# A graph layer's main loop: 108 instead of 96 chunks of edges summed on TensorE, by a schedule made at build time

## What is computed

```python
h = relu(layernorm(x))
xw = h @ W_in
W_ij = (shifted_softplus(edge_attr_20 @ W_f1 + b_f1) @ W_f2 + b_f2) * edge_weight1
x_ij = xw[dst] * W_ij
out = segment_sum(x_ij, src, 6250)
return x + shifted_softplus(out @ W_o1 + b_o1) @ W_o2 + b_o2
```

## Time and profile before

| | before |
|---|---|
| median of 3 runs | 2446.28 us (2439.71 to 2447.08) |
| the profiled execution | 2439.41 us, span 2437.6 us |
| busy, share of the span: PE, POOL, DVE, ACT | 87%, 79%, 73%, 71% |
| chain of work that ended last | DMA of the scatters 42%, POOL 22%, issue 21%, PE 8%, DVE 4% |
| scatters | 1180, of 1592 ns on average |
| mean granted TensorE clock | 0.966 of full speed |

### The profile page before, as it was taken

One profiled execution on the slowest core, in us unless ns is written; L12 is line 12 of the kernel. 1 busy time (PEld: TensorE's weight loads), 2 busy tenths in 40 slices (PEclk: granted clock), 3 DMA queues, 4 the chain that ended last, 5 costly groups with the idle time before them and its releaser, 6 DMA issues.

```text
span 2437.6 us, 54860 instructions
## 1 busy us (share of the span) xinstructions
PE 2132.0 (87%) x15903; PEld 1381.0 (57%) x16098; DVE 1790.4 (73%) x3773; ACT 1737.7 (71%) x4085; POOL 1935.9 (79%) x1240
## 2 busy tenths in 40 slices
PE   2688999999999998999999999999999999999935
PEld 1555556665556565555556555565565565555613
DVE  8667777777777777777777777777777777777747
ACT  1577777777777777777777777777777777777703
POOL 2388888888888888888888888888888888888863
PEclk9889999999999999999999999999999999999968
DMA  8366666666556665666566666565566566666564
GB/s 350 109 96 90 87 90 91 87 94 90 86 92 90 86 94 87 88 92 87 88 92 90 84 93 90 85 93 90 84 92 90 86 90 91 87 90 92 76 169 172
DMA packets 360143, 244.45 MB, mean 100 GB/s; under 512 B 90419, under 2 KB 347137, under 8 KB 359711
## 3 DMA queue, kind: packets, MB, share of 16 engines
q0 software_dynamic: 170912, 80.62, 35.4%
q1 hardware_dynamic: 187715, 159.83, 24.9%
q10 hardware_dynamic: 1212, 0.42, 0.1%
HBM read 141.43 MB, written 99.27 MB: 99 GB/s over the span
## 4 chain that ended last, share of the span: by engine, by line
DMA 42%; POOL 22%; issue 21%; PE 8%; DVE 4%; ACT 1%; POOLq 0%; ACTq 0%; SPq 0%; DVEq 0%
DMA acc<-region,target 42%; POOL acc L591 21%; PE ps L1276 2%; PE ps L1295 2%; PE ps L1255 1%; PE ps L1245 1%; PE ps L1262 1%; ACT region L713 1%; DMA w_f<-in_L_gnn_W_f_dram 1%; PE ps L1326 0%; POOLq L590 0%; DVE region L1150 0%; DVE mean L853 0%; DVE variance L861 0%; DVE region L1165 0%
## 5 line engine op out<-in xcount | busy, mean ns | idle before, releaser
L591 POOL DMA_INDIRECT acc<-region,target x1180 | 1878.8, 1592 | 376.6 <-issue 267.0
L1276 PE MATMUL ps<-region 128*128 128x386 bf16 x2688 | 580.9, 337 | 71.1 <-ACT region L722 70.4
L722 ACT ACTIVATE region<-ps 128x386 bf16<-128x386 f32 x672 | 331.6, 493 | 231.6 <-PE ps L1276 195.5
L1295 PE MATMUL ps<-region 64*128 64x448 bf16 x4032 | 453.4, 358 | 17.9 <-DVE region L1067 13.4
L745 ACT ACTIVATE region<-ps,cut_col 128x128 f32<-128x128 f32 x1564 | 440.3, 363 | 0.6 <-PE ps L1326 0.6
L1255 PE MATMUL ps<-w_f,region 128*128 128x128 f32 x3128 | 428.8, 282 | 13.1 <-issue 2.4
L1255 PEld LDWEIGHTS ps<-w_f,region 128*128 128x128 f32 x3128 | 427.8, 198 | 12.1
L1276 PEld LDWEIGHTS ps<-region 128*128 128x128 bf16 x2688 | 232.4, 97 | 315.6 <-ACT region L722 109.7
L1002 DVE SCALAR_TENSOR_TENSOR region<-ps,bf_negative,region 128x512 f32<-128x512 f32 x391 | 291.3, 745 | 123.8 <-ACT region L708 84.0
L993 DVE TENSOR_SCALAR moved<-region,weight_limit,spare_row 128x4 f32<-128x4 f32 x295 | 97.3, 330 | 374.3 <-ACT region L713 247.4
L1262 PE MATMUL ps<-region 128*128 128x129 f32 x2360 | 327.4, 279 | 28.9 <-DVE region L1002 24.5
(11 more groups left out here) (128 smaller groups left out, 1690.6 us busy)
## 6 DMA issues: line engine op xcount, KB each, us to landing
dst_b<-dst_rows SPq DMA_DIRECT2D x391, 128.0 KB
src_b<-src_rows SPq DMA_DIRECT2D x295, 128.0 KB
acc<-region,target POOLq DMA_INDIRECT x1180
attrT<-in_edge_attr_dram SPq DMA_DIRECT2D x782, 20.0 KB
acc<-region SPq DMA_DIRECT2D x20, 640.0 KB, 17.4
xwin<-xw_parts SPq DMA_DIRECT2D x391, 31.5 KB
region<-acc SPq DMA_DIRECT2D x48, 256.0 KB, 4.7
xw_parts<-parts SPq DMA_DIRECT2D x12, 384.0 KB, 2.3
```

What stands on the lines that cost most here:

```text
L591: nc.gpsimd.indirect_dma_start(out=acc[a], out_offset=bass.IndirectOffsetOnAxis(ap=target[:, slot, t:t + 1], axis=0), in_=summed[:, slot, ...
L722: nc.scalar.activation(binned[:, h, j, :], binned_ps[:, 0:PC], ACT.Copy).then_inc(s_binned, 1)
L1276: ins = MM(binned_ps[:, 0:PC], place[:, h % 2, t, j * P:(j + 1) * P], payload_high[:, h % 2, t, :], start=(t == 0), stop=(t == T - 1))
L1295: ins = MM(ps[6 + r][:, 0:NL], binned[rows, slot, j, part * F:(part + 1) * F], in_node[rows, i, slot, :], start=(d == every[0] and part == ...
```

## The change

The period becomes 25 chunks with seven of them on PE, cut off at 108, of which the last is chunk 384. The distances between PE chunks are 3 and 4 in turn. 283 pool chunks are left of 295. The fixed tables give way to a loop that runs while the kernel is built and assigns every sort, one-hot, half node sum and add to a step: at most two sorts per step (one early, one late; `late` is a sort's position), at most one half of a node sum, its one-hots two steps ahead, and the add one step behind the second half. A sort comes no sooner than 3 steps after its chunk and after its slot is free. The place matrices come two at a time. `in_node` takes turns by the number of the tile, and `local_f` shares the memory of `bin_i`. The order of each engine's code within a step stays.

```diff
-U = 16
-ON_PE = (3, 7, 11, 15)
+U = 25
+ON_PE = (2, 6, 9, 13, 16, 20, 24)
+NPE = 108
...
-        BINNED_AT = {4: (0,), 5: (1, 2), 6: (3, 4), 7: (5, 6)}
         OLD, NEW = (3, 2), (1, 0)
-        NODES_AT = ((4, 0, OLD), (5, 0, NEW), (6, 1, OLD), (7, 1, NEW))
-        DENSE_AT = ((6, 0, OLD), (7, 0, NEW), (8, 1, OLD), (9, 1, NEW))
-        ADDED_AT = ((8, 0), (10, 1))
-        PLACED_AT = ((0, (0,)), (2, (1,)), (3, (2, 3)))
-        LAST_DENSE = max(pe_index) + DENSE_AT[1][0]
-        EXTRA = 2 * (SLOTS - 1)
+        PLACED_AT = ((0, (0, 1)), (2, (2, 3)))
+        SORTS_PER_STEP = 2
...
+        def tiles_summed(kk):
+            return range(2 if kk % SLOTS < SLOTS - 1 else 1)
+
+        sorts_at, nodes_at, sums_at, adds_at = ({} for _ in range(4))
+        sorted_in, summed_in = {}, {}
+        turn, last = (0, 0), 0
+
+        def next_turn(t):
+            return (t[0], 1) if t[1] == 0 else (t[0] + 1, 0)
+
+        for kk in range(NPE + SLOTS - 1):
+            for i in range(JT if kk < NPE else 0):
+                j = tile_of(kk % SLOTS, i)
+                earlier = kk - ((kk - 1 - j // 2) % SLOTS + 1)
+                freed = (summed_in[earlier, j % 2], 1) if kk >= SLOTS else (0, 0)
+                turn = max(next_turn(turn), (pe_chunks[kk] + 3, 1), freed)
+                sorted_in[kk, i] = turn
+                sorts_at.setdefault(turn[0], []).append((kk, kk % SLOTS, i, turn[1]))
+            for i in tiles_summed(kk):
+                for ages in (OLD, NEW):
+                    for d in ages:
+                        if holds(kk, d):
+                            step, late = sorted_in[kk - d, place_of((kk - d) % SLOTS, tile_of(kk % SLOTS, i))]
+                            ready = max(ready, step + 2 + late) if d != ages[0] and holds(kk, ages[0]) else step + 2 + late
+                    if any(holds(kk, d) for d in ages):
+                        last = max(last + 1, ready)
+                        nodes_at.setdefault(last - 2, []).append((kk, kk % SLOTS, i, ages))
+                        sums_at.setdefault(last, []).append((kk, kk % SLOTS, i, ages))
+                summed_in[kk, i] = last
+                adds_at.setdefault(last + 1, []).append((kk, kk % SLOTS, i))
...
-                    for kk, h, i in dense_jobs(k, ADDED_AT, 1):
+                    for kk, h, i in adds_at.get(k, ()):
...
-                    for job in dense_jobs(k, DENSE_AT, 0):
+                    for job in sums_at.get(k, ()):
                         add_nodes(*job)
-                    for job in jobs[1:]:
-                        bin_up(*job)
+                    for kk, h, i, late in jobs:
+                        if late:
+                            bin_up(kk, h, i)
```

More of the change, by code:

```diff
@@ L35, in gnn_kernel @@
     LN2 = math.log(2.0)
-    NU = NCH // U
-    NPE = NU * len(ON_PE)
     NL = N // BINS
@@ L42, in gnn_kernel @@
     PC = 3 * F + 2
-    NQU = len(ON_PE)
     BANK_QCS = NPE // 3
     assert all((n >> 6) * SEVENTH >> 11 == n // NL for n in range(N))
-    assert N == BINS * NL and NL % 64 == 0 and NL <= 512 and NPE % 4 == 0 and NPE == 3 * BANK_QCS and BANK_QCS * BINS <= 512
-    assert NQU % SLOTS == 0 and JT == 2 * SLOTS - 1
+    assert N == BINS * NL and NL % 64 == 0 and NL <= 512 and NPE == 3 * BANK_QCS and BANK_QCS * BINS <= 512
+    assert JT == 2 * SLOTS - 1
     acc = [nc.dram_tensor(f"acc{t}", (ACC_ROWS, F), fp32, kind="Internal").ap() for t in range(ACCS)]
@@ L101, in gnn_kernel @@
         pe_src, bin_i, bit_i = (region1[:, 2 * G * CE + k * NPE * T:2 * G * CE + (k + 1) * NPE * T].bitcast(i32).rearrange("p (n t) -> p n t", t=T) for k in range(3))
-        bin_f, local_f = (region1[:, 2 * G * CE + k * NPE * T:2 * G * CE + (k + 1) * NPE * T].rearrange("p (n t) -> p n t", t=T) for k in range(3, 5))
-        assert 5 * NPE * T <= G * CE
+        bin_f = region1[:, 2 * G * CE + 3 * NPE * T:2 * G * CE + 4 * NPE * T].rearrange("p (n t) -> p n t", t=T)
+        local_f = bin_i.bitcast(fp32)
+        assert 4 * NPE * T <= G * CE
         region2 = sb("region2", [P, max(NB * F, 4 * ACCS * EB * F, 14 * CE + 6 * T)])
@@ L294, in known @@
             return type(c) is int
-        pe_index = {c: kk for kk, c in enumerate(c for c in range(NU * U) if c % U in ON_PE)}
+        pe_chunks = [c for c in range(NCH) if c % U in ON_PE][:NPE]
+        pe_index = {c: kk for kk, c in enumerate(pe_chunks)}
+        assert len(pe_chunks) == NPE
         pe_counts = [0] + list(itertools.accumulate(int(c in pe_index) for c in range(NCH)))
@@ L355, in sums_until @@
             return JT * (kk // SLOTS) + 2 * (kk % SLOTS) + i + 1
[L357 to L377, removed]
@@ L382, in nodes_until @@
+        c = last
+        LAST_STEP = max(NCH + 1, c + 2)
         def nodes_until(kk, i, ages):
             behind = [d for d in OLD + NEW if d < ages[-1]]
-            jobs = [(q, r) for q in range(kk + 1) for r in range(2 if q < kk else i + 1) if 2 * (q % SLOTS) + r < JT]
+            jobs = [(q, r) for q in range(kk + 1) for r in tiles_summed(q) if q < kk or r <= i]
             return sum(1 for q, r in jobs for d in OLD + NEW if holds(q, d)) - sum(1 for d in behind if holds(kk, d))
         def hybrid_steps(step):
-            for c in range(-2, max(NCH + 2, LAST_DENSE + EXTRA + 3)):
+            for c in range(-2, LAST_STEP + 1):
@@ L731, in step @@
                         take_sums(n % 4)
-                    jobs = binnings(k)
-                    for job in jobs[:1]:
-                        take_binned(*job)
+                    jobs = sorts_at.get(k, ())
+                    for kk, h, i, late in jobs:
+                        if not late:
+                            take_binned(kk, h, i)
                     n = k + 1
@@ L910, in bins @@
                 for r, k in enumerate(ON_PE):
-                    last = V.tensor_copy(pe_src[:, :, :].rearrange("p (u r) t -> p u r t", r=len(ON_PE))[:, :, r, :],
-                                         src_int[:, 0:NU * U, :].rearrange("p (u k) t -> p u k t", k=U)[:, :, k, :])
+                    n = len(range(r, NPE, len(ON_PE)))
+                    last = V.tensor_copy(pe_src[:, r:NPE:len(ON_PE), :], src_int[:, k:k + (n - 1) * U + 1:U, :])
                 link(last)
@@ L1059, in step @@
                             places(k - off, tiles)
-                    for kk, h, i, ages in dense_jobs(k, NODES_AT, 0):
+                    for kk, h, i, ages in nodes_at.get(k, ()):
                         j = tile_of(h, i)
@@ L1066, in step @@
                                 wait(dve, s_binned, (kk - d) * JT + place_of(slot, j) + 1)
-                                V.tensor_scalar(in_node[:, i, slot, :], counting[:, 0:NL], binned[:, slot, j, 3 * F:3 * F + 1],
+                                V.tensor_scalar(in_node[:, sums_until(kk, i) % 2, slot, :], counting[:, 0:NL], binned[:, slot, j, 3 * F:3 * F + 1],
                                                 binned[:, slot, j, 3 * F + 1:PC], ALU.subtract, ALU.is_equal).then_inc(s_node, 1)
@@ L1294, in add_nodes @@
                             rows = slice(r * CAP, (r + 1) * CAP)
-                            ins = MM(ps[6 + r][:, 0:NL], binned[rows, slot, j, part * F:(part + 1) * F], in_node[rows, i, slot, :],
+                            ins = MM(ps[6 + r][:, 0:NL], binned[rows, slot, j, part * F:(part + 1) * F], in_node[rows, sums_until(kk, i) % 2, slot, :],
                                      start=(d == every[0] and part == 0), stop=(d == every[-1] and part == 2))
```

## The result

| | before | after |
|---|---|---|
| median | 2446.68 us (4 runs, 2439.71 to 2447.84) | 2495.85 us (4 runs, 2490.62 to 2496.93) |
| the profiled execution | 2439.41 us, span 2437.6 | 2496.54 us, span 2494.7 |
| busy: PE, POOL, DVE, ACT | 87%, 79%, 73%, 71% | 89%, 75%, 74%, 71% |
| scatters | 1180 | 1132 |

The changed kernel is slower by 49.2 us: ratio 1.0203, 95% interval 1.0179 to 1.0227. The forecast was 2481, its range 2455 to 2525.

What follows compares the result with a forecast made beforehand. PE was taken to bound the loop instead of POOL: profiled 2439.4 us, + 36.1 for the loop, + 3 half clock, + 3 prologue, - 4 tail = 2477.5; with half of the 6.9 median offset 2481, range 2455 to 2525.

Steps and rivals of the forecast that it cites:

- What bounds: Main loop: POOL's scatters bound before, PE after; 370 stretches on PE sum to 2080.5 us without late adds.
- The four kinds of stretch: PE between hidden products: 243 full at 5.69 us, 103 without sums 5.56, 15 one sort fewer 5.3, 9 without node sum 5.07.
- The added wait: PE's node sum waits 1.2 us for an add to accT behind DVE's payload, 51 times, 61 us; bounds 1.0 and 1.5.
- The drain: DVE between payload and add: the rows show no pause, so the sum leaves out the skill's rule of about 0.8 us.
- E: Rival: DVE pauses behind the two long payload instructions, 0.8 us more per wait, 2522 us; chance 0.02.
- Half clock: PE at 1.2 GHz after waits: two cases of 1.6 each, 3 us; bounds none and all 51 (82 us).
- Prologue and tail: Before and after the loop: VectorE's bin and rank work adds 3 us, the tail takes 4 off (bounds 0 and 9).
- The sum: Whole kernel: profiled execution 2439.4 + 36.1 + 3 + 3 - 4 = 2477.5 us, then half of 6.9 for the median: 2481.
- A: Rival: the add to accT is not late, as DVE begins earlier or PE's node sum is late too; 2420 us, chance 0.10.
- C: Rival: POOL still bounds, with PE faster in full steps than read; 2355 us, chance 0.03.
- D: Rival: a bin of 14 holds more than 64 edges of a chunk, so the general branch runs; unpriced, chance 0.01.
- One sign: Expected in the changed profile: ACT's L712 no longer waits for acc; no size given.

Runs made afterwards that it cites:

- e5: e1 with the fourth scatter of every pool chunk left out on POOL: 2426.10 us, where e1 has 2426.47.
- e6: Kernel before with the fourth scatter of every pool chunk left out: 2357.34 us, ratio 0.9659 to the kernel before.
- e1: Changed kernel with the adds to accT moved ahead of the payload in DVE's step: 2426.47 us, ratio 0.9944 to the kernel before.
- e3: Changed kernel with the adds to accT one place later, behind the comparison of duplicates: 2570.09 us (two runs).
- e4: Changed kernel with the adds ahead of the payload only for PE chunks of even running number: 2467.84 us, ratio 1.0117 to the kernel before.
- e2: Kernel before with the adds to accT moved ahead of the payload, as a control: 2441.53 us, ratio 1.0005.
- e7: e1 with 102 chunks on PE, four of every 15: 2426.06 us, ratio 0.9937 to the kernel before.
- e9: e1 with the early sort behind the hidden product in steps without same-source sums: 2424.30 us, ratio 0.9935 to the kernel before.

## Why the prediction was right, and where its sizes were off

**What bounds.** POOL before, PE after: right, by e5 and e6. PE's need in the loop, without the late adds, was put at 2080.5; the changed kernel's 2160.8 less 51 x 1.50 is 2084.3. The four kinds of stretch held: 5.70 for 5.69, 5.55 for 5.56, 5.02 for 5.07, and 5.53 for the 5.3 that I had taken between two ends.

**The added wait.** Right in place, cause and count: 51 in the 370 stretches, and e1, e3 and e4 move the time with it. The size was put at 1.2, upper bound 1.5, and measured 1.50 (7.053 - 5.553), so 76.5 us instead of 61.2. This term alone makes most of the miss. Its parts: L1002 starts 0.11 behind the hidden product in all 51, as taken; from there to the add 2.23 us (on average, 2.07 to 2.43) for the 2.07 read from one case; the add 1.08, as taken; and 0.15 from its end to PE's first matmul, which I had put into the bound and not into the value. The 2.07 was the shortest: over the 96 payload steps of the kernel before the same chain takes 2.07 to 2.46, 2.16 on average. One row for a chain of short instructions was too thin.

**The drain.** E, by which DVE would pause 0.8 us more ahead of the add, would have made the wait 2.3 with the measured rest. The rows show none: in the stretch above L1051 starts at 368.60, 0.03 behind the end of L1049, lasts 0.69, and L1060 starts at 369.21. E took one sentence of the Trainium skill (VectorE: DVE Perf Modes, The DRAIN you can't avoid) alone; the same paragraph adds that a next instruction that isn't held back starts earlier. The trace agrees with that for L1060, which starts 0.08 before L1051's end.

**Half clock.** Taken as 3 us, was 0 in the 370 stretches. e3 shows that the mechanism is there. The prediction's reading that none ran at half clock behind a wait up to 1.36 was wrong: five stretches without a node sum did, which began with waits of 0.29 to 1.08, each with another wait of 0.83 to 1.31 in the stretch before it. One of them, on PE in the kernel before, where the filter product takes 1.91 instead of 1.05:

```profile
596.22 0.70 PE L1245 MATMUL ps<-attrT,w_f 20*128 20x256 f32 x4 [1.08 <-ACT region L712]
...
597.67 1.91 PE L1255 MATMUL ps<-w_f,region 128*128 128x128 f32 x8 [0.22 <-issue]
```

The other premise, that the new wait of 1.2 lies under the 1.42 where the clock began to fall, went with the size of the wait: 26 of the 51 are 1.42 or longer. That the clock held in all 51 is luck as far as the prediction goes.

**Prologue and tail.** +3 was +7.0 up to step 16. The first hidden product of the loop comes at 98.40 instead of 92.29. The three steps on 1512 instead of 1344 columns (the prediction had two) account for 2.1 us (4 x 0.17 each); I had bounded the whole at 5. The value is itself unsteady: that product comes at 92.1 to 92.4 in the four traces with 96 chunks on PE, and at 96.4 to 98.4 in the six with 108. Where the rest comes from is open. The tail gave 5.1 for the 4 taken, though e2, with the tail of the kernel before, is 2.0 longer there than that kernel, so a us or two is chance. The early gain of the scatters was lost to the reload of x, as said: L1140, the former L1131, ran from 2417.42 to 2424.11, and the tail's first add began at 2424.15 behind it.

**The sum.** +36.1 + 3 + 3 - 4 = 38.1 was forecast between the profiled executions, and 57.1 measured: 15.3 from the size of the wait, 3.8 from the other stretches, 4.0 from the prologue, less 3 for the clock and 1.1 for the tail. The 3.4 that the forecast added from profiled execution to median did not come: the median of after lies 0.7 below its profiled execution. Rivals A and C fell with L1060's waits and POOL's slack. D did not happen. One sign came only in part: ACT's L719 (L712 before) still waits 90 times for a scatter from 300 to 2200 us, but 0.4 at most, where it had waited up to 3.2.

## What to carry to other kernels

When a schedule is made by a program, the order inside a step is part of it: the old tables kept the adds out of the payload's step, and the new loop, which counts only what PE does per step, lost that unwritten rule. Read the old distances for what they avoid, step by step on every engine, before replacing them. And when work moves from the bounding engine to the next, compare the limits first: the kernel before had 3.4% to give by e6, but moving 12 chunks to PE brings only 13.4 us of it (e1), which 51 waits of 0.26 us would use up. The version of e1, one block of code moved, takes 0.9944 of the time before (0.9927 to 0.9961); e7 and e9 lie within its interval.

## What the runs showed of the hardware

DVE's short instructions vary with POOL. L1002 on 128x4 elements, minimum, median and maximum in ns:

```profile
L1002 DVE TENSOR_SCALAR moved<-region,weight_limit,spare_row x283: 286/290/620, 118.7 to 2387.6; 128x4 f32<-128x4 f32 x142
```

Sorted by how long before it the latest scatter had started, in bins of 0.2 us, it took 0.51 on average (up to 0.62) when that was 0.4 to 0.6 us ago, in 59 cases, 0.34 when it was 0.6 to 0.8 (64 cases), and 0.29 in every other bin. The kernel before has 0.53 (35 cases) and 0.33 (28) there, and 0.29 to 0.32 elsewhere. This would fit the Trainium skill (SBUF — State Buffer, SBUF: two separate sides), by which VectorE and GpSimd share a pair of ports that one of them holds at a time; but the page limits this to certain modes and operands, and no run here tells whether L1002's are among them. It is a correlation within two profiles; I made no run to separate it.

When the clock falls is not told by the length of one wait. In the kernel before it fell in 10 of the 16 stretches that began with 1.42 us or more, and not in the other six, whose waits go up to 1.83; and it fell in the five named above, behind two shorter waits. Behind a wait of 1.40 for ACT's copy, in a stretch without a node sum, it fell once of 18 in the kernel before and seven times of 25 in e7. In e3 it fell behind waits of 1.89 to 2.20, nine times of 51. It fell in none of the changed kernel's 51 stretches with a wait of 1.28 to 1.63 and a second of 0.58. What decides is open.
